# Square roots of the moduli taken for up to four sequences in one ScalarE operation, and the residual addition of the softmax over queries moved one step later

## What is computed

```python
x = x + attn_a(ln(x))          # causal, 16 heads of 8 features
x = x + modulus(ln(x))         # sqrt((h @ cos(A))**2 + (h @ sin(B))**2)
x = x + attn_b(ln(x))          # not causal, rotary position code
x = x + modulus(ln(x))
x = x + linear_attention(ln(x));  x = x + mlp(ln(x))
x = x + fp4_ffn(ln(x))
# the softmax over queries:
qkv = x_n @ W.T + b;  q, k, v = split(qkv)
a = softmax(q @ k.T / 128, axis=queries);  x = x + a @ v
x = x + fp4_ffn(ln(x))
```

## Time and profile before

| | |
|---|---|
| median of 3 runs | 2023.92 us |
| the profiled execution | 2022.12 us, its span 2020.4 us |
| TensorE matmuls busy | 1686.0 us |
| VectorE busy | 1410.2 us |
| ScalarE busy | 1056.4 us |
| GpSimd busy | 520.4 us |
| mean granted clock of TensorE | 0.948 of full |

### The profile page before, as it was taken

The page is one execution under the profiler, slowest core; times in us unless marked ns, Lnnn a source line. Parts: engine busy times, 40 slices in busy tenths (PEclk is TensorE's granted clock), DMA queues, the critical chain, the costliest instruction groups (busy, mean ns, idle before and its releaser), DMA issues. The chain is left out here.

```text
span 2020.4 us, 36743 instructions
## 1 busy us (share of the span) xinstructions
PE 1686.0 (83%) x12704; PEld 941.8 (47%) x12781; DVE 1410.2 (70%) x4005; ACT 1056.4 (52%) x1727; POOL 520.4 (26%) x579
## 2 busy tenths in 40 slices
PE   3788888888988989888699999999997866688566
PEld 1233333333333333232366767767675645445454
DVE  6677777788777877775266667766674588655787
ACT  1466666656666666666354544445442355333453
POOL 5455555553333223300100000000002422200222
PEclk9799999999999999999699999999998988789798
DMA  5434332222221122200000000000000000000000
GB/s 95 58 62 96 61 65 49 49 47 46 48 48 24 25 48 48 40 9 1 0 1 2 2 2 2 2 3 1 2 2 1 1 0 0 1 0 0 6 16 21
DMA packets 56691, 49.82 MB, mean 25 GB/s; under 512 B 9221, under 2 KB 54469, under 8 KB 56517
## 3 DMA queue, kind: packets, MB, share of 16 engines
q1 hardware_dynamic: 53692, 46.45, 12.2%
q10 hardware_dynamic: 2824, 1.11, 0.4%
HBM read 7.10 MB, written 2.10 MB: 5 GB/s over the span
## 5 line engine op out<-in xcount | busy, mean ns | idle before, releaser
L500 ACT ACTIVATE at_probs<-ps 128x1024 f32<-128x1024 f32 (+1 forms) x448 | 427.6, 962 | 279.7 <-PE ps L613 273.7
L757 DVE TENSOR_REDUCE at_M<-ps 128x1 f32<-128x512 f32 x512 | 336.7, 686 | 109.5 <-PE ps L589 108.7
L589 PE MATMUL ps<-at_KS,at_QS 96*128 96x512 bf16 (+3 forms) x1024 | 321.8, 352 | 53.5 <-DVE at_M L752 21.0
L752 DVE CUSTOM_DVE_ANT_0 at_masked<-ps,at_mask_row 128x384 bf16<-128x384 f32 (+3 forms) x512 | 228.9, 486 | 74.9 <-PE ps L589 72.8
L630 PE MATMUL ps<-at_probs,at_V 128*9 128x512 f32 (+3 forms) x2048 | 233.0, 527 | 27.1 <-ACT at_C L508 12.3
L613 PE MATMUL ps<-at_QS,at_KS 128*128 128x512 bf16 x947 | 242.9, 343 | 15.1 <-DMA at_QS<-at_nmT 7.5
L589 PEld LDWEIGHTS ps<-at_KS,at_QS 96*128 96x128 bf16 x1024 | 91.6, 98 | 334.6 <-DVE at_M L757 150.7
L380 POOL TENSOR_SCALAR_AFFINE_SELECT at_probs<-at_probs 128x256 f32<-128x256 f32 (+1 forms) x192 | 93.9, 492 | 179.8 <-ACT at_probs L500 178.9
L613 PEld LDWEIGHTS ps<-at_QS,at_KS 128*128 128x128 bf16 x1024 | 93.2, 99 | 83.1 <-issue 25.2
L839 POOL TENSOR_TENSOR la_rstd<-la_vare,mhalf 128x4 f32<-128x4 f32 x16 | 16.1, 1008 | 414.7 <-DVE la_vare L834 414.7
L1250 DVE SCALAR_TENSOR_TENSOR la_phiq<-ps,la_ezq 128x512 f32<-128x512 f32 x64 | 44.2, 690 | 111.8 <-ACT la_ezq L1101 111.8
(11 more groups left out here) (258 smaller groups left out, 3373.7 us busy)
## 6 DMA issues: line engine op xcount, KB each, us to landing
at_QS<-at_splitq SPq DMA_DIRECT2D x288, 64.0 KB
at_KS<-at_splitk SPq DMA_DIRECT2D x279, 64.0 KB
out<-X SPq DMA_DIRECT2D x8, 256.0 KB, 2.3
at_QS<-at_nmT ACTq DMA_DIRECT2D x64, 8.0 KB
at_KS<-at_splitk ACTq DMA_DIRECT2D x9, 64.0 KB
w_raw<-fp_weights SPq DMA_DIRECT2D x1, 560.0 KB, 5.7
w_wv<-L_attn_a_wv SPq DMA_DIRECT2D x1, 512.0 KB, 6.8
w_wo<-L_attn_a_wo SPq DMA_DIRECT2D x1, 512.0 KB, 6.6
```

Of the source, the lines that this page charges most:

```text
L500: act.activation(v(probs[u % 4][:]), v(src), ACT.Exp, scale=layers[layer(n)]["scale"])\
L589: last = pe.matmul(ps[:, FIRST + U % 2, o * stride:o * stride + width], QS[n % 2][0:SHIFT_AT, h, qt * P:(qt + 1) * P], KS[n % 2][0:SHIFT_A ...
L752: last = v.tensor_tensor_reduce(masked[U % 4][:, o * stride:o * stride + width], src[:, o, :], mask_row[:, 512 - width:512], 1.0, 4 * NEG, ...
L757: v.tensor_reduce(M[gq % 2][:, heads[0]:heads[-1] + 1, qt], src, AX.X, ALU.max).then_inc(max_free, 1)
```

## The change

Two edits that do not touch each other.

**Roots in groups.** `m_total` becomes a list of four tiles, one for each item modulo `ROOTS` = 4; the tiles for `angle` and `turns` move to make room, and GpSimd waits once for the waves before it writes over `angle`. `root_group` gives for each item the first and last item of its group: (0, 3), (4, 7), (8, 11), (12, 14), and item 15 alone. `mroot` now exists only for the last item of a group, at the same due time as before; it takes the root of all tiles of the group in one operation (128 x 2048, for the fourth group 128 x 1536). The additions to X of the group's items follow, one each 0.4 units. The number of square roots computed stays the same.

**Addition one step later.** `query_softmax` gets a fifth stage ADD. VectorE adds item s-4 in step s, behind the normalisation of item s-1 and ahead of the statistics of item s. With five stages the count of whole steps that would go into the hardware loop falls below four, so `run_steps` writes all steps out.

```diff
--- before.py
+++ after.py
@@ -83,6 +83,16 @@
 SHIFT_ROWS = 2
 SHIFT_AT = 96
 LAG = 2
+ROOTS = 4
+
+
+def root_group(n, items):
+
+    first = n - n % ROOTS
+    last = min(first + ROOTS, items) - 1
+    if last == items - 1:
+        return (n, n) if n == last else (first, last - 1)
+    return first, last
...
         at(r + 1.95, "mtotal", n)
-        at(r + 2.25, "mroot", n)
-        at(r + 2.65, "madd", n)
+        lo, hi = root_group(n, 2 * seqs)
+        if n == hi:
+            at(r + 2.25, "mroot", n)
+            for i in range(hi - lo + 1):
+                at(r + 2.65 + 0.4 * i, "madd", lo + i)
     for i in range(late_loads):
         at(5.0 + 0.6 * i, "load", 0, 0, i)
     return [event[2:] for event in sorted(found)]
...
-    angle, turns = [spare[:, 20 + 2 * i:22 + 2 * i].rearrange("p a c -> p (a c)") for i in range(2)]
+    m_total = [spare[:, 16 + 4 * i:20 + 4 * i] for i in range(ROOTS)]
+    angle, turns = [spare[:, 28 + 2 * i:30 + 2 * i].rearrange("p a c -> p (a c)") for i in range(2)]
...
@@ -387,16 +401,18 @@
         def m_sum(n, q, gq, i):
 
             g.wait_ge(misc_free, uses_of_misc("mpart", n, 0, 1))
+            if n == ROOTS - 1:
+                g.wait_ge(waves_ready, 1)
             for half in range(2):
-                last = g.tensor_tensor(m_total[:, 2 * half:2 * half + 2], m_squares[half][:, :, 0:P],
+                last = g.tensor_tensor(m_total[n % ROOTS][:, 2 * half:2 * half + 2], m_squares[half][:, :, 0:P],
                                        m_squares[half][:, :, P:2 * P], ALU.add)
             last.then_inc(m_total_ready, 1)
 
         def m_add(n, q, gq, i):
             b = n % seqs
             xs = X[:, 4 * b:4 * b + 4, :]
-            g.wait_ge(m_length_ready, n + 1)
-            g.tensor_tensor(xs, xs, m_total, ALU.add).then_inc(m_added, 1)
+            g.wait_ge(m_length_ready, root_group(n, items)[1] + 1)
+            g.tensor_tensor(xs, xs, m_total[n % ROOTS], ALU.add).then_inc(m_added, 1)
...
         def lengths(n, q, gq, i):
-            act.wait_ge(m_total_ready, n + 1)
-            act.activation(m_total, m_total, ACT.Sqrt).then_inc(m_length_ready, 1)
+            lo, hi = root_group(n, items)
+            act.wait_ge(m_total_ready, hi + 1)
+            some = spare[:, 16 + 4 * (lo % ROOTS):20 + 4 * (hi % ROOTS)]
+            act.activation(some, some, ACT.Sqrt).then_inc(m_length_ready, hi - lo + 1)
...
+    MEASURE, PROJECT, SCORE, SUM, ADD = range(5)
...
@@ -1405,6 +1423,11 @@
                 n, p = s - PROJECT, (par - PROJECT) % 2
                 wait(v, misc_full, 4 * (n - 1) + 1)
                 apply(v, n, xn[p], tiles(X, n, per), p).then_inc(xn_ready, 1)
+            if on(ADD):
+                n, p = s - ADD, (par - ADD) % 2
+                xs = tiles(X, n, per)
+                v.wait_ge(out_ready, n + 1)
+                v.tensor_tensor(flat(xs), flat(xs), ps[:, OUT + p, :], ALU.add).then_inc(out_free, 1)
             if on(MEASURE):
                 measure(v, tiles(X, s, per), par)
             if on(SCORE):
@@ -1426,12 +1449,7 @@
                 v.reciprocal(inverse[p][:], total[p][:])
                 v.drain()
                 v.tensor_tensor(vs[p][:], val[p][:], over(inverse[p][:], 2, P), ALU.mult).then_inc(vs_ready, 1)
-            if on(SUM):
-                n, p = s - SUM, (par - SUM) % 2
-                xs = tiles(X, n, per)
-                v.wait_ge(out_ready, n + 1)
-                v.tensor_tensor(flat(xs), flat(xs), ps[:, OUT + p, :], ALU.add).then_inc(out_free, 1)
-        run_steps(v, items, 4, step, before=1)
+        run_steps(v, items, 5, step, before=1)
```

More of the change, by code:

```diff
@@ L234, in attention_stream @@
     spare = core["X1"]
-    m_xn, m_total = spare[:, 0:4], spare[:, 4:8]
-    m_xT = spare[:, 8:12].rearrange("p a c -> p (a c)")
-    m_squares = [spare[:, 12 + 4 * i:16 + 4 * i].rearrange("p a c -> p (a c)").rearrange("p (t c) -> p t c", t=2)
+    m_xn = spare[:, 0:4]
+    m_xT = spare[:, 4:8].rearrange("p a c -> p (a c)")
+    m_squares = [spare[:, 8 + 4 * i:12 + 4 * i].rearrange("p a c -> p (a c)").rearrange("p (t c) -> p t c", t=2)
                  for i in range(2)]
-    angle, turns = [spare[:, 20 + 2 * i:22 + 2 * i].rearrange("p a c -> p (a c)") for i in range(2)]
+    m_total = [spare[:, 16 + 4 * i:20 + 4 * i] for i in range(ROOTS)]
+    angle, turns = [spare[:, 28 + 2 * i:30 + 2 * i].rearrange("p a c -> p (a c)") for i in range(2)]
     m_stats = sb("m_stats", [P, 4, 6])
@@ L1328, in query_softmax @@
     vs_ready, out_ready, out_free = sem("vs_ready"), sem("out_ready"), sem("out_free")
-    MEASURE, PROJECT, SCORE, SUM = range(4)
+    MEASURE, PROJECT, SCORE, SUM, ADD = range(5)
     def gpsimd(g):
@@ L1334, in step @@
                 root(g, s, par)
-        run_steps(g, items, 4, step, before=1)
+        run_steps(g, items, 5, step, before=1)
     def scalar(act):
@@ L1357, in step @@
                                    scale=SCALE, accum_out=total[p][:, t:t + 1]).then_inc(E_ready, 1)
-        run_steps(act, items, 4, step, before=1)
+        run_steps(act, items, 5, step, before=1)
     def tensor(pe):
@@ L1397, in step @@
                 last.then_inc(out_ready, 1)
-        run_steps(pe, items, 4, step, before=1)
+        run_steps(pe, items, 5, step, before=1)
     def vector(v):
```

## The result

The changed kernel takes 1974.68 us in the median of four runs (1972.55 to 1977.68), against 2022.47 us of the kernel before beside it: ratio 0.9763, 95% interval 0.9738 to 0.9787. So the kernel is 2.0 to 2.4% faster, 41 to 48 us by the medians, where 35.4 us were forecast. The first measurement lies under the range given, which ended at 1978 us; the second lies inside it.

The account below looks back on a forecast made before the run. TensorE was taken as the bound, waiting for ScalarE's roots and table loads. Stream 31.7 - 6.3 = 25.4 us plus softmax 10.0 gave 35.4 us off, 1988 us on the median; own range 1981 to 1994, wider range 1978 to 2002 us.

Parts of the forecast that it names:

- items 8, 9, 10 and 12: Second attention, roots removed: 8.1 us of TensorE waits and 6.3 us of clock falls go, together 14.4 us.
- Item 13: Near the stream's end, root removed: of a 2.77 us wait about 0.5 stays, so 2.2 us gained.
- The kept groups: Longer roots of items 3, 7, 11 and 14 add 4.7 us of TensorE wait, item 7's clock fall 1.57: 6.3 us cost.
- I cost them at nothing: GpSimd's additions in the stream, 1.27 us each, priced at zero; uncovered they would cost 19 us.
- the same addition disappears from that place for the ungrouped items: One reason for pricing GpSimd's additions in the stream at zero; the other was stacks loaded most of an item ahead.
- 5 x (1.57 + 1.23) = 14.0 us: Causal part, items 0, 1, 2, 4, 5: TensorE's waits for the copies of maxima and keys both go, 14.0 us.
- Item 6: At the border of the layers, root removed: only the wait of 1.12 us counted as gained.
- the causal part takes its share back: Rival, chance 0.12: VectorE and GpSimd's maskings pace the causal part, nothing of its 15.1 us survives; 2003.6 us.
- Idle times of this size are not followed by a fall of the clock ..., so three falls go: Softmax over queries: with border idle time of about 1.0 us, three clock falls go, 3 x 1.57 = 4.7 us.
- The loop written out saves register work I cannot see on TensorE: zero: Softmax over queries: writing all steps out instead of a hardware loop was priced at zero.
- The term of the moved addition: Softmax over queries: normalisation starts 1.06 us sooner at each of five borders, 5.3 us gained.
- all of ScalarE's freed time counts: Rival, chance 0.09: loads 28.2, roots' fixed cost 2.2, clock falls 4.7, softmax 10.0: 45.1 us gained, 1979 us.

Follow-up runs that it names:

- the small roots: Changed kernel plus a one-column square root at each of the eleven vacated places, bringing both table loads back: 2007.81 us, ratio 0.9928 to the kernel before.
- the second trace of the changed kernel: The changed kernel measured once more, unaltered, against the kernel before: 1979.66 us, ratio 0.9800 (0.9784 to 0.9816).

## Why the prediction was right and wrong

**Right: the sign, the main cause and the second attention.** TensorE waited for ScalarE because of the loads and the root, and each removed set gave it back. For items 8, 9, 10 and 12 the forecast was 3.6 us each; the stretches fell from 64.55 to 60.82 us, 3.7. By the small roots, 1.7 us of it are the loads, 0.4 the root's width, and 1.6 the fall of the clock, which came with the wait of 2.02 us and not with that of 1.57. Item 13 was 2.2 in the forecast; the work behind it moved up by 2.3. The load went into the sum at its row's 1283 ns. By the Trainium skill, ScalarE: Activation LUTs, section What ACT_TABLE_LOAD costs, two switches would take ScalarE 5.3 us, an estimate from its 2.66 us for one. The traces of this case don't agree: each load beside a root starts within 0.02 us of the end of the instruction before it, no drain shows, and a pair around a root of 203 ns cost TensorE 2.5 us. The kept groups cost 1.28, 1.28 and 0.86 us of wait, as estimated, and item 7's got its fall of the clock.

**Wrong: "I cost them at nothing."** The step that failed is the price of GpSimd's additions. The forecast said that "the same addition disappears from that place for the ungrouped items" and drew no gain from it. In the causal part GpSimd's splits and maskings follow each other closely, and 1.27 us more among them make TensorE wait twice for a masking. The kernel before shows it behind item 3's root, a few us after the two waits of the earlier trace rows:

```profile
303.69 1.27 POOL L399 TENSOR_TENSOR X<-X 128x512 f32<-128x512 f32 x1
...
305.38 0.83 PE L630 MATMUL ps<-at_probs,at_V 128*9 128x384 f32 x8 [0.62 <-POOL at_probs L380]
...
308.32 0.62 PE L630 MATMUL ps<-at_probs,at_V 128*9 128x256 f32 x8 [0.52 <-POOL at_probs L380]
```

These 1.14 us could have been priced ahead of the result; the changed kernel has neither wait where no addition stands. The term of items 0, 1, 2, 4 and 5, "5 x (1.57 + 1.23) = 14.0 us", measures 5 x 4.2 = 21 us: 2.5 for the loads, 1.0 to 1.2 for the addition's place (put back in the changed kernel, and taken out of the kernel before), and about 0.4 us for the root's own width, as the wait of 1.14 us beside the small root shows. (Item 4 gave 4.2 us in the second trace of the changed kernel and 2.7 in the first, which has a fall of the clock late in that stretch.) Item 6 gave 2.2 us instead of 1.1, since I had counted one of its two waits (1.12 us) and left out the other, 0.77 us for the copy of the maxima. Item 3's group costs 2.3 us instead of 1.28, with the wait of 0.95 us for a masking, the same mechanism the other way round. The rival in which "the causal part takes its share back" was wrong in direction: that part gave more than its waits for ScalarE.

**Near sum, wrong reason: the softmax.** The forecast was 10.0 us and 11.3 were measured. "Idle times of this size are not followed by a fall of the clock ..., so three falls go" credited the shorter wait with the clock. And "mostly not either" was too hopeful: of the kernel before's six waits of 1.57 us behind causal items, three were followed by a fall. The written-out loop alone keeps the clock at 1.00 with 1.81 us idle at each border. Whether the shorter wait would have done so too with the loop in place, no run tells, as none moves the addition and keeps the loop. "The loop written out saves register work I cannot see on TensorE: zero" is the step that failed here: it was worth 5.8 to 6.4 us, falls included. That the sum still came out near is luck, since the falls stood in it under another cause. The term of the moved addition, 5.3 us, measured 5.3. Why the loop's 0.15 us a step decide over the clock is open: in the stream too, waits of the same 2.02 us were followed by a fall or not.

**Chance.** The first measurement's 47.8 us and the second's 41.1 lie around the 44.5 us that the forecast makes with the terms above corrected: 35.4 + 7.0 + 1.1 - 1.0, and 0.7 more for the second attention with item 13, and 1.3 for the softmax. Stages without an edit differ by 4 to 6 us between traces, and the stretch of the second item, ahead of the first root, was 47.9 to 52.8 us long in kernels that are equal up to there. The lower end of the range, built on the rival in which "all of ScalarE's freed time counts", left no room for what GpSimd would give on top.

## What to carry to other kernels

Price a removed operation on every engine that leaves its place with it: here a quarter of a causal stretch's gain came from GpSimd's addition that moved along with the root. Where an in-order engine serves a busier one in small jobs, work costs nothing in its pauses (here) and most of itself ahead of a job that is waited for (1.0 to 1.2 of 1.27 us); moving it or a wait without such a pause only changes the releaser. And when a reorder also changes how a loop is built, run the loop alone: here it was more than half of one edit's gain.

## What the runs showed of the hardware

- A square root of 2048 columns takes 1909 ns, of 1536 columns 1482, of 512 columns 629 and of one column 203.
- A table load takes 1283 ns, and a root behind it starts 0.01 us later.
- TensorE's granted clock depends on more than the last wait: 2.02 us idle were followed by 3.4 us at 0.50 in some stretches and not in others of the same kernel, 1.80 to 1.81 us between written-out steps in none of ten, 1.88 to 2.14 us between looped steps in three of five, and 1.57 us in three of the six causal stretches of the kernel before.
- Such a fall costs 1.6 us where TensorE is the bound. Where TensorE waits for ScalarE right after, it cost nothing in the earlier trace rows, but 0.9 us in two other kernels (a causal stretch of 50.6 us for 49.7 with the loop written out, and item 1's 49.9 us with the addition in a pause, where 49.0 were due).
